# First cross-attention with keys on the partitions: scores in two passes, the maximum per query as a contraction row, no transposes of the exponentials

## What is computed

```
xn = layernorm(layernorm(x));  q = (xn @ w_q) in 16 heads of 64
k, v = split(context @ w_kv) in 16 heads of 64
attn = softmax(q * 64**-0.5 @ k.T)      # per head 128 x 12544
x = x + tanh(gate) * (concat_h(attn @ v) @ w_out + b_out)
```

## Time and profile before

| | |
|---|---|
| runs of the kernel, us | 1468.83, 1468.99, 1470.45; median 1468.99 |
| the profiled execution, us | 1469.13 |
| its span, first to last instruction, us | 1467.4 |
| mean granted TensorE clock | 0.941 of full |
| busy share of the span | PE 87%, PEld 61%, DVE 71%, ACT 54%, POOL 39% |
| TensorE instructions | 10912 matmuls |

### The profile page before, as it was taken

How to read it: one execution, slowest core, us unless ns; L and a number is a source line. 1 busy time by engine, 2 the same in 40 slices (tenths; PEclk the granted TensorE clock), 3 DMA queues, 4 the chain that set the end, 5 groups by cost and what they waited for, 6 DMA issues and landing times. The chain is left out here.

```text
span 1467.4 us, 29268 instructions
## 1 busy us (share of the span) xinstructions
PE 1273.5 (87%) x10912; PEld 894.1 (61%) x10913; DVE 1039.5 (71%) x1976; ACT 798.2 (54%) x1453; POOL 577.3 (39%) x632
## 2 busy tenths in 40 slices
PE   3899999999999999999999999999845987234498
PEld 1466666666666666666766666666633576211297
DVE  5777777777787878787777777777734723699632
ACT  2586667676767676767676767676610042351010
POOL 3163636363636464636363636364200000248000
PEclk9999999999999999999999999999976998566699
DMA  5223232222222222222323232222252743500155
GB/s 207 75 60 79 50 80 50 78 51 78 52 77 52 76 52 77 51 78 51 79 50 79 51 79 51 78 52 51 68 196 80 247 151 99 202 0 0 65 194 196
DMA packets 108262, 126.35 MB, mean 86 GB/s; under 512 B 17424, under 2 KB 96592, under 8 KB 107872
## 3 DMA queue, kind: packets, MB, share of 16 engines
q1 hardware_dynamic: 107312, 121.43, 28.6%
q10 hardware_dynamic: 816, 3.15, 0.6%
HBM read 74.34 MB, written 0.16 MB: 51 GB/s over the span
## 5 line engine op out<-in xcount | busy, mean ns | idle before, releaser
L717 PE MATMUL ps<-ident,p_exp 128*128 128x128 f32 x1568 | 423.0, 273 | 1.7 <-ACT p_exp L420 1.4
L431 ACT ACTIVATE pT_hi<-ps 128x512 f16<-128x512 f32 x448 | 241.9, 540 | 260.1 <-PE ps L717 260.1
L532 DVE TENSOR_REDUCE neg_row<-ps 128x1 f32<-128x896 f32 x224 | 244.5, 1092 | 150.6 <-PE ps L707 146.7
L540 DVE TENSOR_TENSOR pT_lo<-ps,pT_hi 128x512 f16<-128x512 f32 x448 | 277.0, 618 | 59.5 <-ACT pT_hi L431 58.6
L348 POOL CAST k_top<-k_raw 128x448 f16<-128x448 f32 x218 | 123.3, 566 | 358.2 <-ACT k_raw L427 358.2
L420 ACT ACTIVATE p_exp<-ps,neg_max,esc 128x896 f32<-128x896 f32 x224 | 245.7, 1097 | 13.5 <-DVE neg_max L534 8.1
L717 PEld LDWEIGHTS ps<-ident,p_exp 128*128 128x128 f32 x1568 | 221.2, 142 | 40.7 <-ACT k_raw L427 6.9
L350 POOL TENSOR_TENSOR k_rest<-k_raw,k_top 128x448 f16<-128x448 f32 x218 | 226.1, 1037 | 17.7
L733 PE MATMUL ps<-v_hi,pT_hi 128*128 128x65 f16 x1568 | 164.3, 193 | 0.6 <-DVE pT_lo L540 0.6
L734 PE MATMUL ps<-v_lo,pT_hi 128*128 128x64 f16 x1568 | 164.4, 193 | 0.0
L735 PE MATMUL ps<-v_hi,pT_lo 128*128 128x65 f16 x1568 | 163.8, 193 | 0.0
(11 more groups left out here) (312 smaller groups left out, 2030.6 us busy)
## 6 DMA issues: line engine op xcount, KB each, us to landing
k_st<-k_top SPq DMA_DIRECT2D x436, 56.0 KB, 2.0
k_st<-k_rest SPq DMA_DIRECT2D x436, 56.0 KB, 2.0
c_raw<-in_ctxT SPq DMA_DIRECT2D x14, 896.0 KB, 5.3
xa_ct<-in_ctxT SPq DMA_DIRECT2D x14, 896.0 KB, 4.7
xa_cn<-in_ctx SPq DMA_DIRECT2D x14, 896.0 KB, 5.1
me_w<-in_me_w SPq DMA_DIRECT2D x8, 1536.0 KB, 8.1
me_w<-in_me_w SPq DMA_DIRECT2D x8, 768.0 KB, 5.0
ss_b_all<-ss_bc SPq DMA_DIRECT2D x1, 2048.0 KB, 7.1
```

The costliest lines, as they stand in the source:

```text
L431: nc.scalar.activation(pT_hi[:, n % 2, t0:t1, :], s_t[b][:, 0:(t1 - t0) * S].rearrange("p (t s) -> p t s", s=S), ACT.Copy).then_inc(pT_hi_ ...
L532: link(nc.vector.tensor_reduce(neg_row[:, i:i + 1], s_scores, AX.XY, ALU.max, negate=True))
L540: nc.vector.tensor_tensor(pT_lo[:, n % 2, t0:t1, :], s_t[b][:, 0:(t1 - t0) * S].rearrange("p (t s) -> p t s", s=S), pT_hi[:, n % 2, t0:t1, ...
L717: mm = nc.tensor.transpose(s_t[b][:, s * S:(s + 1) * S], p_exp[:, n % 2, tile * P:(tile + 1) * P], ident[:, :])
```

## The change

The scores are computed with the keys on the output partitions (stationary: a 128-key tile of `k_st`; moving: the 128 queries), 7 matmuls of 128 columns in each of two passes.

- `first_pass(n+2)`: high part of the keys with `q_hi`, two steps ahead, in two alternating PSUM areas.
- `tiles_max` (VectorE): maximum over the seven tiles for each of 128 key partitions and 128 queries; `turn_max` (TensorE): one float32 transpose of it; `new_max` (VectorE): maximum over 128, then the running maximum in units (`m_col`, float16).
- `lay_max` (TensorE): a matmul with one stationary column that turns `m_col` into a row; `m_row` (ScalarE): copies this row into a free row of `q_low`, against which `k_st` holds the constant -8192.
- `second_pass(n+1)`: low parts, and with that row the subtraction of the maximum, added onto the first pass.
- `exponent` then needs no bias per query, and its output already has the layout that `weigh` takes: the 7 transposes per step fall away. `p_high` (ScalarE) and `p_low` (VectorE) each become one operation over 896 from `p_exp` in SBUF.
- `k_st` holds a second copy of the high part (the DMA of `k_top` writes two places; 12 more DMAs before the loop); `absmax` is cut into quarters; `group_max` computes `drop` for four heads; before the loop GpSimd has more memsets, and the scale of q is made one for all queries by a matmul; all six early key parts must be there before the first scores.

Core of the diff:

```diff
...
-                            sp.dma_start(k_st[(slice(r, r + DH),) + k_place(U, side)], k_top[r:r + DH, b, :]).then_inc(k_placed[b], 16)
+                            sp.dma_start(k_st[(slice(r, r + DH),) + k_places(U, side)],
+                                         k_top[r:r + DH, b, :].unsqueeze(1).to_broadcast([DH, 2, HCH])).then_inc(k_placed[b], 16)
...
                 def exponent(n):
-                    c, h = n // H0, n % H0
-                    act.wait_ge(neg_max_ready, n + 1)
-                    at_least(act, t1_done, n - 1)
-                    nc.scalar.activation(p_exp[:, n % 2, :].rearrange("p (b k) -> p b k", b=2), s_scores, ACT.Exp,
-                                         bias=neg_max[:, c % 2, h:h + 1], scale=esc[:, c % 2:c % 2 + 1]).then_inc(exp_done, 1)
+                    act.wait_ge(scores_done, n + 1)
+                    at_least(act, pT_lo_ready, n - 1)
+                    nc.scalar.activation(p_exp[:, n % 2, :], s_scores[n % 2], ACT.Exp, bias=ln_k[:, 0:1],
+                                         scale=esc[:, n // H0 % 2:n // H0 % 2 + 1]).then_inc(exp_done, 1)
+
+                def m_row(n):
+                    h = n % H0
+                    r = DH * (1 - h % 2)
+                    act.wait_ge(m_row_done, n + 1)
+                    nc.scalar.activation(q_low[r:r + 1, h, :], s_max[n % 2][0:1, :], ACT.Copy).then_inc(m_row_ready, 1)
...
-                def turned(n, b):
-                    t0, t1 = ((0, T0), (T0, TILES))[b]
-                    nc.scalar.activation(pT_hi[:, n % 2, t0:t1, :], s_t[b][:, 0:(t1 - t0) * S].rearrange("p (t s) -> p t s", s=S),
-                                         ACT.Copy).then_inc(pT_hi_ready, 1)
+                def p_high(n):
+                    act.wait_ge(exp_done, n + 1)
+                    at_least(act, pv_done, n - 1)
+                    nc.scalar.activation(pT_hi[:, n % 2, :, :].rearrange("p t s -> p (t s)"), p_exp[:, n % 2, :], ACT.Copy).then_inc(pT_hi_ready, 1)
...
                     c, h = n // H0, n % H0
+                    p_high(n)
                     if n and v_at(n - 1):
                         v_high(*v_at(n - 1))
-
-                    at_least(act, pv_done, n - 1)
-                    act.wait_ge(t0_done, n + 1)
-                    turned(n, 0)
+                    if n + 1 < NT:
+                        m_row(n + 1)
+                    if n + K_AHEAD < NT:
+                        k_copy(n + K_AHEAD)
                     if n + 1 < NT:
                         exponent(n + 1)
-                    act.wait_ge(t1_done, n + 1)
-                    turned(n, 1)
-                    if n + K_AHEAD < NT:
-                        k_copy(n + K_AHEAD)
                     if 6 <= h <= 9 and c + 1 < NCH:
                         c_high(c + 1, h - 6)
...
-                def row_max(n):
-                    c, h = n // H0, n % H0
-                    i, par = n % 2, c % 2
-                    v.wait_ge(scores_done, n + 1)
-                    link(nc.vector.tensor_reduce(neg_row[:, i:i + 1], s_scores, AX.XY, ALU.max, negate=True))
-                    link(nc.vector.tensor_scalar(neg_new[:, i:i + 1], neg_row[:, i:i + 1], esc[:, par:par + 1], LN_K, ALU.mult, ALU.add))
-                    nc.vector.tensor_tensor(neg_max[:, par, h:h + 1], neg_new[:, i:i + 1], neg_max[:, 1 - par, h:h + 1],
-                                            ALU.min).then_inc(neg_max_ready, 1)
-
-                def p_low(n, b):
-                    t0, t1 = ((0, T0), (T0, TILES))[b]
-                    v.wait_ge(pT_hi_ready, n * 2 + b + 1)
-                    nc.vector.tensor_tensor(pT_lo[:, n % 2, t0:t1, :], s_t[b][:, 0:(t1 - t0) * S].rearrange("p (t s) -> p t s", s=S),
-                                            pT_hi[:, n % 2, t0:t1, :], ALU.subtract).then_inc(pT_lo_ready, 1)
+                def tiles_max(n):
+                    v.wait_ge(first_done, n + 1)
+                    nc.vector.tensor_reduce(tile_max[:, n % 2, :], s_scores[n % 2].rearrange("p (t s) -> p s t", s=S), AX.X,
+                                            ALU.max).then_inc(tile_max_done, 1)
+
+                def new_max(n):
+                    c, h, i = n // H0, n % H0, n % 2
+                    m = m_col[:, c % 2, h:h + 1]
+                    v.wait_ge(max_turned, n + 1)
+                    link(nc.vector.tensor_reduce(raw_max[:, i:i + 1], s_turned(n), AX.X, ALU.max))
+                    if c == 0:
+                        nc.vector.tensor_scalar(m, raw_max[:, i:i + 1], 1.0 / M_UNIT, None, ALU.mult).then_inc(m_ready, 1)
+                    else:
+                        nc.vector.scalar_tensor_tensor(out=m, in0=raw_max[:, i:i + 1], scalar=1.0 / M_UNIT, in1=m_floor[:, h:h + 1],
+                                                       op0=ALU.mult, op1=ALU.max).then_inc(m_ready, 1)
+
+                def group_max(c, g):
+
+                    par, hs = c % 2, slice(4 * g, 4 * g + 4)
+                    at_least(v, decay_ready, c * 4 + g - 3)
+                    v.wait_ge(m_ready, c * H0 + 4 * g + 4)
+                    link(nc.vector.tensor_scalar(run_max[:, par, hs], m_col[:, par, hs], m_unit[:, par:par + 1], None, ALU.mult))
+                    nc.vector.tensor_tensor(drop[:, hs], run_max[:, 1 - par, hs], run_max[:, par, hs], ALU.subtract).then_inc(drop_ready, 1)
+                    f = c * 4 + g + 1
+                    if 4 <= f < NCH * 4:
+                        par, hs = f // 4 % 2, slice(4 * (f % 4), 4 * (f % 4) + 4)
+                        link(nc.vector.tensor_scalar(m_floor[:, hs], run_max[:, 1 - par, hs], m_per[:, par:par + 1], None, ALU.mult))
+
+                def p_low(n):
+                    v.wait_ge(pT_hi_ready, n + 1)
+                    nc.vector.tensor_tensor(pT_lo[:, n % 2, :, :].rearrange("p t s -> p (t s)"), p_exp[:, n % 2, :],
+                                            pT_hi[:, n % 2, :, :].rearrange("p t s -> p (t s)"), ALU.subtract).then_inc(pT_lo_ready, 1)
...
                     if n + 1 < NT:
-                        row_max(n + 1)
+                        new_max(n + 1)
+                    p_low(n)
                     if n and v_at(n - 1):
                         v_low(*v_at(n - 1))
-                    p_low(n, 0)
+                    if h % 4 == 2:
+                        group_max(c, h // 4)
                     if h % 4 == 1 and n > 1:
                         flush(n // 4 - 1)
+                    if h == 15 and c + 2 < NCH:
+                        absmax(c + 2, 0)
                     if c + 1 < NCH:
-                        if h in (2, 3):
-                            absmax(c + 1, h - 2)
+                        if h in (0, 1, 3):
+                            absmax(c + 1, (1, 2, 0, 3)[h])
                         if h == 4:
                             scale(c + 1)
                             unscale(c + 1)
...
-                    p_low(n, 1)
+                    if n + 2 < NT:
+                        tiles_max(n + 2)
...
-                def scores(n):
-                    h = n % H0
+                def first_pass(n):
+                    h, i = n % H0, n % 2
                     if n < K_AHEAD:
                         pe.wait_ge(k_early, 4 * (n // 2) + 4)
                     elif n % 2 == 0:
                         pe.wait_ge(k_placed[0], k_turn(n))
                         pe.wait_ge(k_placed[1], k_turn(n + 1))
-                    at_least(pe, exp_done, n)
-                    for k, q in enumerate((q_hi, q_lo)):
-                        for b in range(2):
-                            mm = nc.tensor.matmul(s_scores[:, b, :], q[:, h, :], k_st[:, n // 2 % 4, n % 2, b * HCH:(b + 1) * HCH],
-                                                  start=(k == 0), stop=(k == 1))
+                    at_least(pe, exp_done, n - 1)
+                    for tile in range(TILES):
+                        mm = nc.tensor.matmul(s_scores[i][:, tile * S:(tile + 1) * S], k_st[:, n // 2 % 4, i, 0, tile * P:(tile + 1) * P],
+                                              q_hi[:, h, :], start=(tile % T0 == 0), stop=True, skip_group_check=True)
+                    mm.then_inc(first_done, 1)
+
+                def turn_max(n):
+                    pe.wait_ge(tile_max_done, n + 1)
+                    if n > 2:
+                        first, f = (n - 2) % 4 == 0, (n - 2) // 4
+                        at_least(pe, flushed, 2 * (f - 1 if first else f))
+                    nc.tensor.transpose(s_turned(n), tile_max[:, n % 2, :], ident[:, :]).then_inc(max_turned, 1)
+
+                def lay_max(n):
+                    c, h = n // H0, n % H0
+                    pe.wait_ge(m_ready, n + 1)
+                    nc.tensor.matmul(s_max[n % 2][0:1, :], m_col[:, c % 2, h:h + 1], ident16[:, :], start=False, stop=True,
+                                     skip_group_check=True).then_inc(m_row_done, 1)
+
+                def second_pass(n):
+                    h, i = n % H0, n % 2
+                    if n == 0:
```

(37 more changed lines are left out.)

160 lines of the change are left out of this document (98 added, 62 removed).

## The result

The changed kernel takes 1487.59 us (median of four runs, 1484.54 to 1490.74) against 1469.01 for the kernel before (1468.83 to 1470.45). The ratio is 1.0124, 95% interval 1.0101 to 1.0148: slower by 1.24%, 18.6 us. The forecast was 1476.6, so +7.5, with more chance for slower than for faster; the sign was the likelier one, the time lies in the range, and the size is short by 11 us.

The account below looks back on a forecast made before the run. TensorE's stream was taken to bound the old kernel; a TensorE-VectorE loop plus extras and collisions gave 72.6 us a chunk against 72.7 (-2 over 14 chunks). With +6 before and +3.5 in the last: +7.5, 1476.6 us, range 1400 to 1520.

Parts of the forecast that it names:

- Passes: TensorE's two score passes in each step: seven 128-column matmuls each, 0.056 us a matmul, 0.78 for both.
- TensorE 4.01: TensorE's own work in a step with values: 4.01 us, with `lay_max` counted at 0.06.
- the loop 4.12: Step set by a loop over TensorE and VectorE, from one `turn_max` to the next: 4.12 us, 65.9 a chunk.
- Collisions of 5.0 a chunk: In the loop, VectorE's `p_low` and `drop` held up by GpSimd at the shared SBUF port: 5.0 us a chunk.
- The forecast's own sign: Sign against the forecast: if `p_low`'s mean stays under 1.2 us, it is wrong and the time is 1407 to 1441.
- Scale at head 4, 0.7: VectorE's seven tiny linked scale operations at head 4 exceed the loop's slack by 0.7 us a chunk.
- Quantisation, 1.0 on average: VectorE's quantisation pieces in six chunks exceed the loop's slack, about 1.0 us a chunk on average.
- Before the loop, +6: Ahead of the loop, the first value projection now waits for keys and the first turn, from 46.05 to 52.3: +6 us.
- I cost at nothing: GpSimd's added memsets before the loop: no cost, taken as hidden by the loads and VectorE's work there.
- Last chunk +5.5 for +3.5: Heads 8 to 15 of the last chunk, without value projection: about 3.7 us a step before, now 4.12, so +3.5.
- Late keys: Slower rival, 14%: `first_pass` waits for keys that come late; four steps of 16 waiting 1 us more give 1533.
- The faster case: Rival, 32%: GpSimd and `p_low` seldom meet in the loop; a chunk of 67.6 to 70, total 1407 to 1441 us.

Follow-up runs that it names:

- e2: Changed kernel with VectorE's tile maximum over 4 of the 7 key tiles from step 2 on (work left out): 1439.99 us.
- e1: Changed kernel with TensorE transposing the tile maxima twice from step 2 on: 1508.73 us.
- e3: Changed kernel with GpSimd's `k_rest` covering 32 of 448 columns (work left out): 1464.54 us.
- e4: Changed kernel with, before the loop, the first value projection ahead of the first score pass and `tiles_max(1)` behind the second value remainder: 1480.54 us.
- e13: Changed kernel with GpSimd's four fills of `k_st` behind the split of the first context chunk, not at the start: 1484.52 us.
- e14: The edits of e12 and e13 together: 1496.40 us.
- e17: e10 with VectorE's extras behind the tile maxima as in e16 and the fills of e13, first pass in its old place: 1475.51 us.
- e10: e4 plus GpSimd's key split before its decay wait, two bound matmuls for four, VectorE's unscale and quantisation behind the tile maxima: 1456.36 us.
- e16: e12 with VectorE's group maxima, flush and column maxima behind the tile maxima of their step: 1436.88 us.
- e8: Changed kernel with GpSimd splitting the keys before it waits for the decay in every fourth step: 1481.56 us.
- e12: e10 with TensorE's first pass ahead of the weighing and the second pass: 1497.18 us.

## Why the prediction was right in sign and short in size

Of the 14 us between the forecast's +7.5 and this execution's +21.6, 7.9 lie ahead of chunk 1, 2.3 in the steady chunks, 2.0 in the last chunk and 1.9 behind it.

**Passes, right.** Seven matmuls in 0.39, 0.056 each.

**TensorE 4.01 and the loop 4.12: mis-sized, both by 0.19.** They measured 4.20 (e2) and 4.31. The term is "`lay_max` 0.06", in fact 0.25. In the loop, the turn that had to wait takes 0.17, not 0.11, and from the end of the first pass to the next turn it is 1.35, not 1.41, so these two cancel. (The forecast's own terms, 2.65 + 0.26 + 1.09 + 0.1, add up to 4.10, not 4.12.) That it is a loop over two engines is shown by e1 (+0.11 for 0.11 to 0.17 added) and e2. For 223 steps 0.19 is 42 us.

**Collisions of 5.0 a chunk: mis-sized the other way.** The mechanism is there: `p_low`, behind a late GpSimd operation, takes 0.78 more, and `drop` 0.30. But the forecast counted nine `p_low` that might be caught, and two are, one of which costs nothing. The runs show 1.2 in a plain chunk, and by e3 2.3 in one with quantisation, where `k_rest` catches the quantisation piece and the one-column `m_col` (0.96 for 0.16), which the forecast didn't have. The forecast's own sign ("wrong if `p_low`'s mean stays under 1.2, then 1407 to 1441") came true and the time did not follow, since the loop's extra 3.1 a chunk had taken its place. A steady chunk was forecast as 65.9 + 0.7 + 5.0 = 71.6 ahead of the quantisation, and measured 71.4 as 16 × 4.31 = 69.0, and 1.0 in interval 5, 1.2 in interval 11, 0.2 elsewhere. Two errors of more than 3 us cancelled: that the steady state came out right is luck.

**Scale at head 4, 0.7:** 1.0 measured, for bound and scale together; the change's two additional bound matmuls were left out of the sum. **Quantisation, 1.0 on average:** 2.7 in most of the chunks that have it, some 17 in all, 1.2 on average, and by e3 about half of it is collisions.

**Before the loop, +6: the step that failed.** +11.5 at step 1's new maximum (59.16 to 70.62), +13.9 at chunk 1. The order: the sum was worked out to the first value projection, and what stands behind it was taken as unchanged; `tiles_max(1)` behind seven value remainders, and the value projections behind the first pass, are 3.7 to 4.4 at step 1 (e4), the lower clock there included. The fills that "I cost at nothing": 1.2 to 2.0 (e13, e14, e17), and the condition named for them held, since they lock the layer norm. The bound's additional matmuls: 0.7 (66.20 in e4, 65.55 in e10). With all three mended step 1's new maximum comes at 64.24 (e17), +5.1. So the forecast's +6 could be had, but by another order than the one it was worked out for. The last 2.4 lie in chunk 0 itself, which the sum took as plain: interval 1 takes 5.27 at a clock of 0.76, interval 7 5.31 with `drop` at 0.92, and interval 10 5.31 with a `p_low` of 1.86.

**The ends.** Last chunk +5.5 for +3.5. The forecast's steps of 4.12 took no account of the clock, 0.50 in the last ones of the changed kernel, while the kernel before kept 1.00 there. The last four intervals took 4.97 to 5.27, at 4.31 they would have been 3.5 shorter; in other executions (e4, e13) some of them took 3.8. So this part is one execution's, and between 2 and 5.5. For the +1.9 behind the last new maximum the clock is no reason, it is nearly the same in both (0.79 and 0.78).

**The rivals.** Late keys fell: no wait of TensorE for the keys' DMA is among those of 220 to 1040 us. The faster case was to decide as soon as collisions stayed below 4.4 a chunk. They did, at 1.2 to 2.3, and the kernel was slower all the same: the case, like the forecast, stood on a loop of 4.12. e16 lies within its 1407 to 1441, with 1437, but by another order of TensorE's and VectorE's work, not by that case's mechanism alone.

On the shared port, the trace of before gave 0.55 for 0.16; now there is more of it, with fills too. The layer norm's `tensor_scalar` waits for a fill (3.39 for 0.41), while the `tensor_tensor` behind it, with two SBUF inputs, takes its 0.43 beside the next fill. The Trainium skill (SBUF — State Buffer, Who interferes with whom) says so: `tensor_scalar` and copies can enter two-port modes that need the shared pair, when their operands meet certain conditions, and a two-input operation contends only with a GpSimd instruction that reads SBUF. By that rule, the trace agrees in both; the forecast had applied half of it, to `p_low` and `drop`, and not to the `tensor_scalar` and copies.

## What to carry to other kernels

When a change closes a loop over two engines, count each link of it with what it costs its neighbours, above all a tiny one of another shape than they: 0.19 us in a 4.3 us loop was worth 42 us here. Read where the long instances of an operation stand, and not its mean: `p_low`'s was 5% above its median and hid the one in 16 that cost 0.8 us a chunk. Price the code before and behind the loop like the loop, instruction by instruction, GpSimd's fills among it. And judge an order only with its partners: one move of VectorE's small operations gained 60 us or lost 19, by where another engine's pass stood, because both idle time and the port's collisions move with it.

## What the runs showed of the hardware

- A fill of one partition × 3584 took 3.08 us, as that of 64 partitions did; in that time a VectorE copy of 256 columns took 3.22 instead of 0.29.
- `tensor_scalar` operations of two and four columns, 0.22 to 0.26 elsewhere, take 1.01 to 1.08 beside `k_rest` in e8 and e12: in e12 `m_floor` does so in intervals 3, 7 and 15 of each of the chunks 1 to 12, and in none of their intervals 11.
- A float16 matmul of 128 columns costs 0.056 with a 128×128 stationary operand, and 0.25 with a one-column one amid others, the gap of 0.10 ahead of it included.
- A one-column float32 matmul with a 128×128 stationary operand costs 0.23 (four in 0.92), more than a float16 one of 448 columns (0.19).
- In the last steps TensorE was busy for 4.91 of 8.00 us before, at a clock of 1.00, and for 3.65 of 6.00 after, at 0.50: the same share at either level.
